# Layer 1's attention in a two-layer transformer kernel: overlapped rounds, attention by query tile, split score products

## The reference

```python
h = _layernorm(x) * (1 + ca) + sa
q, k, v = (x @ W.T for W in (Wq, Wk, Wv))    # 16 heads of 128
q, k = _rmsnorm(q, gq), _rmsnorm(k, gk)      # over each head's 128
scores = einsum('bhqd,bhkd->bhqk', q, k) * 128 ** -0.5, causal mask
out = einsum('bhqk,bhkd->bhqd', softmax(scores), v)
x = x + ga * (out @ Wo.T)
x = x + gb * ffn(h2)                         # SwiGLU, weights lut[idx], 256 -> 688 -> 256
```

## Time and profile before

| | |
|---|---|
| median of 3 runs | 1376.28 us (1374.66 to 1379.0) |
| profiled execution, its own time | 1382.27 us |
| profiled execution, its span | 1380.5 us |
| mean granted TensorE clock | 0.942 |
| busy in the span | PE 89%, PE weight loads 69%, DVE 70%, ACT 51%, POOL 40% |

### The profile page before, as it was taken

One profiled execution on the slowest core, in us unless ns is written; L12 is line 12 of the kernel. 1 busy time (PEld: TensorE's weight loads), 2 busy tenths in 40 slices (PEclk: granted clock), 3 DMA queues, 4 the chain that ended last, 5 costly groups with the idle time before them and its releaser, 6 DMA issues.

```text
span 1380.5 us, 24347 instructions
## 1 busy us (share of the span) xinstructions
PE 1231.5 (89%) x7708; PEld 946.4 (69%) x7708; DVE 962.3 (70%) x2821; ACT 707.0 (51%) x1639; POOL 552.5 (40%) x509
## 2 busy tenths in 40 slices
PE   6889888886469999999989999999998999999998
PEld 5435454443447787777877877778786788777787
DVE  5766777765467868778778678686677676675553
ACT  3354645455336456465464565554564654645442
POOL 0200000000038988898889888887802200000000
PEclk9799898888579999999999999999999999999999
DMA  6411011001110002101102001012001100000000
GB/s 216 123 30 46 24 43 55 24 32 62 61 55 23 32 11 101 41 0 41 41 10 91 21 27 39 8 38 96 4 30 62 34 32 23 8 0 1 16 16 31
DMA packets 31893, 56.85 MB, mean 41 GB/s; under 512 B 7096, under 2 KB 23328, under 8 KB 31312
## 3 DMA queue, kind: packets, MB, share of 16 engines
q1 hardware_dynamic: 27696, 42.93, 9.3%
q0 software_dynamic: 2976, 8.90, 2.2%
q10 hardware_dynamic: 1152, 4.19, 0.8%
HBM read 44.23 MB, written 11.66 MB: 40 GB/s over the span
## 4 chain that ended last, share of the span: by engine, by line
PE 54%; DVE 29%; issue 9%; ACT 5%; DMA 1%; SPq 1%; DVEq 0%; ACTq 0%
PE bank L1364 11%; PE bank L1342 7%; PE bank L278 6%; PE bank L280 6%; PE bank L279 6%; DVE qkst L1022 5%; DVE qk L1041 4%; PE bank L1353 4%; PE bank L1332 2%; DVE negmax L968 2%; PE bank L1277 2%; PE bank L1246 2%; DVE negmax L1054 2%; ACT hN L326 2%; PE bank L1264 1%
## 5 line engine op out<-in xcount | busy, mean ns | idle before, releaser
L574 POOL TENSOR_SCALAR gtmp<-gidx,lut 128x344 f32<-128x344 int32 (+2 forms) x210 | 302.8, 1442 | 21.3
L577 POOL TENSOR_TENSOR gacc<-gacc,gtmp 128x344 f32<-128x344 f32 (+2 forms) x210 | 183.4, 874 | 17.5
L1342 PE MATMUL bank<-kT,qT 128*128 128x128 f32 (+3 forms) x512 | 179.8, 442 | 9.4 <-ACT probs L776 9.4
L1364 PE MATMUL bank<-pT,v 128*128 128x128 f32 x1280 | 155.5, 277 | 12.3 <-ACT pT L769 12.3
L776 ACT ACTIVATE probs<-bank,negmax 128x128 f32<-128x128 f32 (+3 forms) x256 | 135.6, 530 | 53.6 <-DVE negmax L1054 50.9
L1054 DVE TENSOR_REDUCE negmax<-bank 128x1 f32<-128x128 f32 (+3 forms) x256 | 123.6, 485 | 54.9 <-PE bank L1343 53.5
L1364 PEld LDWEIGHTS bank<-pT,v 128*128 128x128 f32 x1280 | 148.0, 192 | 16.2 <-DVE oL L1064 14.9
L968 DVE TENSOR_REDUCE negmax<-bank 128x1 f32<-128x512 f32 (+3 forms) x176 | 108.9, 636 | 67.5 <-PE bank L1266 66.6
L1022 DVE BATCH_NORM_STATS2 qkst<-qk 128x6 f32<-128x128 f32 x512 | 110.2, 281 | 61.7 <-issue 61.6
L278 PE MATMUL bank<-wgH,hL 128*128 128x512 f32 x384 | 152.9, 398 | 0.2 <-issue 0.2
L280 PE MATMUL bank<-wgH,hH 128*128 128x512 f32 x384 | 153.0, 399 | 0.0
(11 more groups left out here) (215 smaller groups left out, 2707.2 us busy)
## 6 DMA issues: line engine op xcount, KB each, us to landing
hH<-h_saved SPq DMA_DIRECT2D x16, 512.0 KB, 3.8
hL<-h_saved SPq DMA_DIRECT2D x16, 512.0 KB, 4.8
qst<-q_parts SPq DMA_DIRECT2D x96, 64.0 KB, 2.3
wg<-in_wqkv SPq DMA_DIRECT2D x4, 1536.0 KB, 8.3
gate<-gates POOLq DMA_DIRECT2D x4, 512.0 KB, 7.0
wo<-in_wo SPq DMA_DIRECT2D x4, 512.0 KB, 9.1
out<-x SPq DMA_DIRECT2D x8, 256.0 KB, 2.1
wmod<-in_wmod SPq DMA_DIRECT2D x1, 1536.0 KB, 10.7
```

What stands on the lines that cost most here:

```text
L574: link(pool.tensor_scalar(tmp if j else acc, part, float(j), lut1[0:rows, j:j + 1], ALU.is_equal, ALU.mult))
L577: link(pool.tensor_tensor(acc, acc, tmp, ALU.add))
L1342: pe.matmul(bank[SCORE_BANKS[i % 3]][:, 0:n], qT[:, h, t * P:n], kT[:, h, 0:n], start=True, stop=False)
L1364: last = pe.matmul(bank[7][:, t * P:(t + 1) * P], v1[:, k, h * HD1:(h + 1) * HD1], pT1[:, h % 2, at:at + P], start=(k == 0), stop=(k == t))
```

## The change

The rounds, now numbered `r` from 0 to 15 and unrolled, overlap. Round 0's projections, normalization and transpositions stand before the loop. Then every round runs through 11 slots, one for each unit of `UNITS1`: all four heads of query tile 0, two pairs of heads of tile 1, and single heads of tiles 2 and 3. In the slots the next round's projections (`PROJECT`), this round's output projection by tile (`OUT_SLOT`, the last tile in slot 1 of the next round), and DVE's statistics, chain and normalization for the next round are placed. The next round's transpositions stand after slot 10.

The scores are three float32r products from high and low parts of q and k, which take the place of the float32 `qT` and `kT`; ACT makes the high and DVE the low part (`turned_low`). The probabilities are no longer scaled. The output projection gives each head by itself into one half of bank 4, and DVE multiplies it by that head's 1/sum and adds it up (`summed`); then it is gated and added to x (`gated`), a tile at a time. The input's parts are loaded a round ahead into two pairs of tiles, the output weights into `hN`, and the weight splits are placed in slots. The small memsets that DVE issued before some instructions are gone, and `wraw` lies in `hF`. Of the diff, the new code on which the order of the work hangs (indentation cut by 8 or 12; the functions of the kernel before that it replaces stand above):

```diff
@@ constants
+R1 = NG * NB
+UNITS1 = tuple((t, h, n) for t, n in enumerate((4, 2, 1, 1)) for h in range(0, HG, n))
+GU1 = len(UNITS1)
+LAST1 = {max(u for u in range(GU1) if UNITS1[u][0] == t): t for t in range(QT)}
+UP = 3 * QT
+UQK = 2 * QT
+PROJECT = {0: (0, 1), 1: (2, 3), 2: (4, 5), 3: (6, 7), 5: (8,), 7: (9,), 8: (10,), 9: (11,)}
+OUT_SLOT = {1: QT - 1, 4: 0, 6: 1, 10: 2}
+TURN_BANKS = (3, 4, 2)
+W1 = 3 * KT + HG
@@ build: tiles of layer 1
+wo = hN
+qTH = sb(s1, "qTH", [P, HG, SEQ], F32R)
+kTH = sb(s1, "kTH", [P, HG, SEQ], F32R)
+qTL = sb(s1, "qTL", [P, HG, SEQ], F32R)
+kTL = sb(s1, "kTL", [P, HG, SEQ], F32R)
+v1 = sb(s1, "v1", [P, 2, QT, HG * HD1])
+pT1 = sb(s1, "pT1", [P, 3, HG * P])
+oH1 = sb(s1, "oH1", [P, 2, HG, P], F32R)
+oL1 = sb(s1, "oL1", [P, 2, HG, P], F32R)
+hH1 = sb(s1, "hH1", [P, KT, SEQ], F32R)
+hL1 = sb(s1, "hL1", [P, KT, SEQ], F32R)
@@ block.sync
+load_h1(1)
+load_wo(0)
+for r in range(2, R1):
+    sp.wait_ge(p1_pe, (r - 1) * UP)
+    load_h1(r)
+    if r % NB == 2 and r + NB < R1 + 2:
+        g = r // NB
+        sp.wait_ge(w1_lo, (g + 1) * W1)
+        load_w1(g + 1)
+        load_wo(g + 1)
@@ block.scalar (ACT)
+def turned_high(r, u):
+    act.wait_ge(tr_pe, r * UQK + u + 1)
+    t = u // 2
+    act.activation((qTH, kTH)[u % 2][:, :, t * P:(t + 1) * P],
+                   bank[TURN_BANKS[u % 3]][:, :].rearrange("p (h t) -> p h t", h=HG), ACT.Copy,
+                   scale=1.0 if u % 2 else gqk[:, 2:3]).then_inc(tr_hi, 1)
...
+def split_slot(r, s):
+    g = r // NB
+    if r % NB == NB - 2 and g + 1 < NG and s in (6, 7, 8, 9):
+        split_high(g + 1, (s - 6,))
+    if r % NB == NB - 1 and g + 1 < NG and s in (3, 4):
+        split_high(g + 1, (2 * KT + s - 3,))
+    if r % NB == 0 and s == 2:
+        split_high(g, range(3 * KT, W1))
+for u in range(UP):
...
+for r in range(R1):
+    for s in range(GU1):
+        if r + 1 < R1:
+            for u in PROJECT.get(s - 1, ()):
+                copy_projected(r + 1, u)
+        exponentials(r, s)
+        if s >= 1:
+            copy_turned(r, s - 1)
+        if s - 2 in LAST1:
+            output_high(r, s - 2)
+        split_slot(r, s)
+        if r == R1 - 1 and s == GU1 - 2:
+            act.wait_ge(p1_pe, R1 * UP)
+    if r + 1 < R1:
+        for u in (0, 1):
+            turned_high(r + 1, u)
+    copy_turned(r, GU1 - 1)
+    if r + 1 < R1:
+        for u in (2, 3):
+            turned_high(r + 1, u)
+    output_high(r, GU1 - 1)
+    if r + 1 < R1:
+        for u in range(4, UQK):
+            turned_high(r + 1, u)
@@ block.vector (DVE)
+def turned_low(r, u):
+    t = u // 2
+    hi, lo = ((qTH, qTL), (kTH, kTL))[u % 2]
+    part = slice(t * P, (t + 1) * P)
+    whole = bank[TURN_BANKS[u % 3]][:, :].rearrange("p (h t) -> p h t", h=HG)
+    dve.wait_ge(tr_hi, r * UQK + u + 1)
+    if u % 2:
+        dve.tensor_tensor(lo[:, :, part], whole, f32(hi[:, :, part]), ALU.subtract).then_inc(tr_lo, 1)
+    else:
+        dve.scalar_tensor_tensor(out=lo[:, :, part], in0=whole, scalar=gqk[:, 2:3], in1=f32(hi[:, :, part]),
+                                 op0=ALU.mult, op1=ALU.subtract).then_inc(tr_lo, 1)
...
+def summed(r, t, heads):
+    total = ytmp[:, t % 2, :]
+    for h in heads:
+        n = r * ITEMS + t * HG + h
+        scale = rsum[:, t * HG + h:t * HG + h + 1]
+        if h == 0:
+            dve.wait_ge(exp1, r * GU1 + max(u for u in range(GU1) if UNITS1[u][0] == t) + 1)
+            dve.reciprocal(rsum[:, t * HG:(t + 1) * HG], sums[:, t * HG:(t + 1) * HG]).then_inc(rsum1, 1)
+            dve.wait_ge(rsum1, r * QT + t + 1)
+        dve.wait_ge(y1_pe, n - n % 2 + 2)
+        part = bank[4][:, n % 2 * D:(n % 2 + 1) * D]
+        if h == 0:
+            dve.tensor_scalar(total, part, scale, None, ALU.mult).then_inc(y1_read, 1)
+        else:
+            dve.wait_ge(y1_read, n)
+            dve.scalar_tensor_tensor(out=total, in0=part, scalar=scale, in1=total, op0=ALU.mult,
+                                     op1=ALU.add).then_inc(y1_read, 1)
+def gated(r, t):
+    b = r % NB
+    n = r * QT + t
+    row = x[:, b * QT + t, :]
+    dve.wait_ge(y1_read, n * HG + HG)
+    dve.tensor_tensor(ytmp[:, t % 2, :], ytmp[:, t % 2, :], gate1[:, 0, b, :], ALU.mult).then_inc(y1_gated, 1)
+    dve.wait_ge(y1_gated, n + 1)
+    dve.tensor_tensor(row, row, ytmp[:, t % 2, :], ALU.add).then_inc(x1_add, 1)
+def split_slot(r, s):
+    g = r // NB
+    if r % NB == NB - 2 and g + 1 < NG and s in (7, 8, 9, 10):
+        split_w1(g + 1, slice(s - 7, s - 6))
+    if r % NB == NB - 1 and g + 1 < NG and s in (4, 5):
+        split_w1(g + 1, slice(2 * KT + s - 4, 2 * KT + s - 3))
+    if r % NB == 0 and s == 3:
+        split_w1(g, slice(3 * KT, W1))
+for u in range(UQK):
+    statistics(0, u)
+mean_squares()
+inverse_roots()
+for u in range(UQK):
+    normed(0, u)
+for u in range(UQK):
+    turned_low(0, u)
+for r in range(R1):
+    more = r + 1 < R1
+    for s in range(GU1):
+        maxima(r, s)
+        if more:
+            for u in PROJECT.get(s - 1, ()):
+                if u < UQK:
+                    statistics(r + 1, u)
+        if s - 3 in LAST1:
+            output_low(r, LAST1[s - 3])
+        for at_slot, heads in ((s, (0, 1)), (s - 1, (2, 3))):
+            if at_slot in OUT_SLOT:
+                t = OUT_SLOT[at_slot]
+                if t < QT - 1:
+                    summed(r, t, heads)
+                elif r:
+                    summed(r - 1, t, heads)
+        if s == 3 and r:
+            gated(r - 1, QT - 1)
+        if s == 8:
+            gated(r, 0)
+        if s == 9:
+            gated(r, 1)
+        if more and s == 5:
+            mean_squares()
+        if more and s == 6:
+            inverse_roots()
+        if more and s >= 7:
+            for u in (2 * (s - 7), 2 * (s - 7) + 1):
+                normed(r + 1, u)
+        if not more and s < NORM_PARTS:
+        split_slot(r, s)
+    summed(r, 2, (2, 3))
+    if more:
+        for u in range(4):
+            turned_low(r + 1, u)
+    output_low(r, QT - 1)
+    if more:
+        for u in range(4, UQK):
+            turned_low(r + 1, u)
+    gated(r, 2)
+summed(R1 - 1, QT - 1, range(HG))
+gated(R1 - 1, QT - 1)
+dve.wait_ge(x1_add, R1 * QT)
@@ block.tensor (PE)
+def project(r, u):
+    g = r // NB
+    if u == 0:
+        pe.wait_ge(w1_lo, g * W1 + 2 * KT)
+        pe.wait_ge(h1_loaded[r % 2], (r // 2 + 1) * 32)
+    if u == UQK:
+        pe.wait_ge(w1_lo, g * W1 + 3 * KT)
+    if u or r:
+        pe.wait_ge(p1_act, r * UP + u - 1)
+    t, c = (u // 2, u % 2) if u < UQK else (u - UQK, 2)
...
+def turn(r, u):
+    pe.wait_ge(qk_norm, r * UQK + u + 1)
+    if u >= 3:
+        pe.wait_ge(tr_lo, r * UQK + u - 2)
+    elif r:
+        if u == 0:
+            pe.wait_ge(exp1, r * GU1 - 1)
+        elif u == 1:
+            pe.wait_ge(y1_read, r * ITEMS - HG)
+        else:
+            pe.wait_ge(exp1, r * GU1)
+    for h in range(HG):
+        last = pe.transpose(bank[TURN_BANKS[u % 3]][:, h * P:(h + 1) * P],
+                            qk[:, u // 2, u % 2, h * HD1:(h + 1) * HD1], identf[:, :])
+    last.then_inc(tr_pe, 1)
+def scores(r, u):
+    t, h, heads = UNITS1[u]
+    w = (t + 1) * P
+    own = slice(t * P, w)
+    if u < 2:
+        pe.wait_ge(tr_lo, r * UQK + 6 + u)
+    else:
+        pe.wait_ge(exp1, r * GU1 + u - 1)
+    if t == QT - 1:
+        pe.wait_ge(tr_lo, (r + 1) * UQK)
+    to = bank[2 + u % 2][:, 0:heads * w].rearrange("p (h k) -> p h k", h=heads)
+    for c in range(heads):
+        n = h + c
+        pe.matmul(to[:, c, :], qTL[:, n, own], kTH[:, n, 0:w], start=(c == 0), stop=False)
+        pe.matmul(to[:, c, :], qTH[:, n, own], kTL[:, n, 0:w], start=False, stop=False)
+        pe.matmul(to[:, c, :], qTH[:, n, own], kTH[:, n, 0:w], start=False, stop=False)
+    pe.matmul(to[:, :, own], identb[:, :], maskb[:, :, :].to_broadcast([P, heads, P]), start=False,
+              stop=True).then_inc(s1_pe, 1)
...
+def output(r, t, heads):
+    for h in heads:
+        n = r * ITEMS + t * HG + h
+        if h == 0:
+            pe.wait_ge(o1_lo, r * QT + t + 1)
+                pe.wait_ge(w1_lo, (r // NB + 1) * W1)
+                pe.wait_ge(tr_lo, (r + 1) * UQK)
+            elif t == QT - 1 and r + 1 < R1:
+                pe.wait_ge(tr_lo, (r + 2) * UQK)
+        pe.wait_ge(y1_read, n - n % 2)
+        mm3(pe, bank[4][:, n % 2 * D:(n % 2 + 1) * D], oH1[:, t % 2, h, :], oL1[:, t % 2, h, :],
+            woH[:, h, :], woL[:, h, :], True, True).then_inc(y1_pe, 1)
+def output_slot(r, s, heads):
+    if s in OUT_SLOT:
+        t = OUT_SLOT[s]
+        if t < QT - 1:
+            output(r, t, heads)
+        elif r:
+            output(r - 1, t, heads)
+for u in range(UP):
+    project(0, u)
+for u in range(UQK):
+    turn(0, u)
+for r in range(R1):
+    more = r + 1 < R1
+    for s in range(GU1):
+        scores(r, s)
+        output_slot(r, s, (0, 1))
+        if s >= 1:
+            turn_probs(r, s - 1)
+        if s >= 2:
+            values(r, s - 2)
+        if more:
```

(56 more changed lines are left out.)

345 lines of the change are left out of this document (98 added, 247 removed).

## The result

The changed kernel takes 1516.01 us (median of 4 runs), the kernel before 1377.22 in the same session: a ratio of 1.101, 95% interval 1.0990 to 1.1029. It is 139 us slower. I had forecast slower, but by 34: the number, 1410, and the range up to 1440 are both missed. The changed kernel's took its median, 1516.01 us; the one of the kernel before took 1382.27, 5 above its median, so the traces differ by 134 us.)

What follows compares the result with a forecast made beforehand. TensorE was taken to bound the rounds. Attention: 34 fill + 585.1 busy rounds + 229.7 quiet - 1.4 + 22.6 weight splits + 38 last round = 908 against 874.1 us, +34; forecast 1410 us, own range 1390 to 1425, whole range 1350 to 1440.

Steps and rivals of the forecast that it cites:

- TensorE waits in three places: Walk of one round: TensorE waits 1.6 us in slot 4, 0.6 in slot 6, 1.9 at the end; 4.1 in all.
- First scores near 425: Round 0, which cannot overlap: first scores at 425.7 us, 34 us after 391.7, including 2 us for a low clock.
- End of the round: Transpositions of q and k need banks released by DVE's low part, behind the last sums; TensorE waits 1.9 us.
- The v projection of rounds 3, 7, 11 waits for a split: First v projection, slot 5, waits for DVE's weight splits placed in slots 4 and 5: +3.0 us each time.
- DVE busy for 41 us: DVE's work in a quiet new round: 41.0 us, fitting under TensorE's 48.0, without idle time from slot 5 on.
- Rounds of 52 and 55 us: First score to first score: a quiet round 52.2 us, one with GpSimd running 55.2; under 52 would refute the forecast.
- The gated steps beside GpSimd: DVE's eight gated steps with two SBUF inputs: some 0.25 us more each while GpSimd runs; the skill allows whole-instruction waits.
- Last round: No projections to hide behind: 27.3 us dense, plus 1, 2.5, 3 and 4 for transpositions, first P, holds, last chain: 38.
- B: Rival: narrow score products in slot 0 run at the f32 rate, adding 19 us: 1429 us; chance 0.24.
- A: Rival: the rounds fill, half of the waits go, 50 us a round: 1345 us; chance 0.23.
- C: Rival: no change, 52 us in all rounds because GpSimd's hindrance falls into slack: 1376 us; chance 0.10.
- (D): Rival: more waits in the rounds than the walk found, +2 us a round: 1440 us; chance 0.03.

Runs made afterwards that it cites:

- low_first: The changed kernel with DVE's low part of the head output moved to the head of its slot, before maxima and statistics; 1429.74 us, ratio 1.0366.
- low_last: The changed kernel with DVE's low part of the head output moved behind the two sums of the slot; 1550.97 us.
- project_first: The changed kernel with the next round's projections ahead of the waiting value products in slots 3, 5 and 9, on TensorE's stream alone; 1449.78 us.
- experiment 6: Weight splits moved to where their engine has time, in f32_low_sums_first and in its twin with split scores; 1381.19 us (ratio 1.0012) and 1392.68 us (ratio 1.01).
- f32_low_sums_first: low_first with DVE's sums also ahead of the statistics, and float32 scores without DVE's low parts of q and k; 1402.72 us.
- low_sums_splits: low_first with DVE's sums also ahead of the statistics and the weight splits moved, split scores kept; 1392.68 us, ratio 1.01.

## Why the prediction was wrong in size

**The step that failed** is the sentence "TensorE waits in three places" of the walk. The list is incomplete. I went through the banks of the output pairs and of the transpositions and left out bank 7, whose release by `o1_lo` the diff shows for `output` and the code for `values` too. Walked by the prediction's own method it would have come out: from the end of slot 3's scores DVE needs 0.2 + 0.47 + 1.76 + 0.67 = 3.1 us to the end of the low part, and TensorE has 0.5 us of transpositions to fill it. The trace has 2.44 of wait. Over the whole span these waits are one row of the page's groups, 83.5 us; the same row of low_first stands under it:

```profile
L1497 PE MATMUL bank<-pT,v 128*128 128x128 f32 x1280 | 185.3, 288 | 83.5 <-DVE oL L1114 83.5
```
```profile
L1497 PE MATMUL bank<-pT,v 128*128 128x128 f32 x1280 | 176.5, 279 | 21.0 <-DVE oL L1114 21.0
```

Low_first, which is the changed kernel as I had walked it, has full rounds of 847.0 us for my 836.0, of 52.8 and 53.7 us without GpSimd and 55.3 to 56.0 with it where no split falls, for my 52.2 and 55.2, and an attention of 921.8 us for my 908. So 86 of the 97 us that the full rounds lacked went with two lines. The direction was no luck: low_first is 51 us slower than the kernel before, at the waits that I had listed. The 20 us between it and my 1410 are 14 of the attention and the 6 that I took off for the profiled execution.

**The clock was missing from the sum.** I charged 2 us for it, in the fill. The granted clock of the full rounds is 0.96 after and was 0.99 before (758.1 us from 446 to 1204.1). With 0.50 in the low stretches that is 8% of 933.4 us, 75 us, against 2%, 15 us (both as rough as the two digits). Products start 0.42 us apart there and 0.23 at full clock, so dense work loses about half of such a stretch: up to 30 us are the clock's. The 28 us of busy time that went in low_first are most of it, and part of the 86 above.

**TensorE's own work was priced low.** The quietest full round has 50.1 us of it (57.7 less 7.6 idle) where I had 48.0, and my terms, with 11 masks for 16, add up to 48.2. The three listed waits were 3.1 us there for my 4.1. So of the 5.6 us that this round lies above my 52.1, the bank has 4.5, TensorE's work 2.1, and the overrated waits take back 1.0.

**Point by point.** *First scores near 425*: 423.0, right; the fill is 32.7 us for my 34. *TensorE waits for DVE's sums at the second output pair*: 1.40 us at 1324.90 for my 1.6, right; the same hold in slot 6 is 0.24 for my 0.6, of which the walk's own 3.4 against 3.0 gave only 0.4. *End of the round*: 0.85 + 0.65 = 1.5 us for my 1.9, right. *The v projection of rounds 3, 7, 11 waits for a split*: 3 waits of up to 2.8 us for my 3.0, right, and moving the splits won 21 to 26 us where I had 22.6 for them as a whole. *DVE busy for 41 us*: 39.5; but *without gaps in slots 5 to 10* does not hold in the changed kernel, where the bank's wait gives DVE idle time; in low_first's last full round its gaps there are 1.07 (before slot 5's maximum), 0.24 and 0.86 us. *Rounds of 52 and 55 us*: wrong, 57.7 in the quietest and up to 68.0. *The gated steps beside GpSimd*: I had 0.25 us more for each. The addition to x (L1144) takes 0.64 us in the mean between 423 and 950 us and 0.42 in the last two full rounds, the product with the gate (L1142) 0.49 and 0.42. It is no even slowing: of those 32 additions 14 took 0.42 us and 10 took 0.83 to 1.04. *Last round*: 38 in the sum, 42.4 measured, and 41.6 even in the best version, so this term was 4 too small.

**The rivals.** B, narrow products at the float32 rate, falls. Score products of 128 columns, start to start 0.11:

```profile
1299.04 0.28 PE L1470 MATMUL bank<-kTH,qTL 128*128 128x128 f32 x1
1299.15 0.27 PE L1471 MATMUL bank<-kTL,qTH 128*128 128x128 f32 x1
1299.26 0.28 PE L1472 MATMUL bank<-kTH,qTH 128*128 128x128 f32 x1
```

The Trainium skill ("TensorE: Matmul & The Clock Gate", section "LDWEIGHTS") puts a weight load at columns / 1.2 ns, by which an estimate for 128 columns is 107 ns. The spacing of these rows is near that, but no run shows that the load sets it, and the profile records 0.19 us for each of their loads. A and C fall with the rounds, and (D)'s "more waits than I found, +2 a round" was the right kind at a third of the size, and had 3 in 100. A walk through five queues is not a thing to trust to 2 us a round.

## What to carry to other kernels

Before the durations of an overlapped schedule are added up, list every PSUM bank and buffer that is reused, with the instruction that releases it, and for each ask what stands ahead of that instruction in its own queue, above all something that waits for the very engine that wants the bank. A release belongs at the head of its slot, ahead of anything that needs the current slot's products. And when an engine is nine tenths busy, what a rewrite can win is the idle tenth: here the most that all mended orders together reached was level.

## What the runs showed of the hardware

**The clock was low where short waits had come close together.** TensorE and the granted clock in round 11 of the changed kernel, first the instructions, then the stretches:

```profile
1139.85 0.39 PE L299 MATMUL bank<-woH,oL 128*128 128x256 f32 x1 [1.40 <-DVE ytmp L1133]
...
1142.76 0.91 PE L1497 MATMUL bank<-pT,v 128*128 128x128 f32 x6 [1.00 <-DVE oL L1114]
1145.66 0.79 PE L299 MATMUL bank<-wgH,hL 128*128 128x512 f32 x1 [2.00 <-DVE wgL L1013]
1146.26 0.63 PE L300 MATMUL bank<-wgL,hH 128*128 128x512 f32 x1
1146.68 0.63 PE L301 MATMUL bank<-wgH,hH 128*128 128x512 f32 x1
```
```profile
1138.00:1141.70 3.70, 2.30 (x17) 1.77 (x16) 2.49 (x9) 1.26 (x3) 0.00 (x0) 1.00 0.00 0
1141.70:1145.00 3.30, 0.96 (x7) 0.74 (x6) 2.99 (x11) 1.05 (x3) 0.00 (x0) 0.98 0.00 0
1145.00:1148.00 3.00, 2.34 (x6) 1.85 (x7) 0.61 (x1) 0.00 (x0) 0.00 (x0) 0.50 0.02 5
```

Behind waits of 1.40, 1.00 and 2.00 us, one soon after the other, the clock stands at 0.50, the lower level of 1.2 GHz, and products of 512 columns start 0.42 us apart (1146.26 to 1146.68), not 0.23. None of the waits is long. By the mean over the full rounds, the clock goes roughly with the idle time of the kernels: 0.93 (low_last), 0.96 (the changed kernel), 0.98 (low_first, project_first), 1.00 (the two of experiment 6). So a wait inside a tuned round cost its length here and, where several fell close together, part of the work that followed: 28 us for 59 us of waits between the changed kernel and low_first. The total of the waits does not fix it: f32_low_sums_first has 0.99 with TensorE idle for 55 us of its full rounds, low_sums_splits 1.00 with 59. And no run changed the clock alone, so that the waits are the cause is argued, not shown.
